# The causal mask of the layer-0 score scan: applied by VectorE while it takes the maximum, in place of a TensorE matmul

## The reference

```python
# layer 0
scores = jnp.einsum('bhqd,bhkd->bhqk', q, k) * hd ** -0.5
scores = jnp.where(jnp.tril(jnp.ones((t, t), bool)), scores, -jnp.inf)
attn = jax.nn.softmax(scores, axis=-1)
x = x + gate * (attn_times_v @ Wproj + bproj)        # then a gelu MLP of width 1024
# layer 1
energy = jnp.einsum('bhqd,bhkd->bhqk', q, k)
att = jax.nn.softmax(energy, axis=-1) / D ** 0.5
out = attn_times_v @ Wp.T + bp + hidden              # then a modulated norm, added
```

## Time and profile before

| what | value |
|---|---|
| median of 3 executions | 1383.65 us (1379.31 to 1385.65) |
| the profiled execution's own time | 1379.89 us |
| its span, first to last instruction | 1378.1 us |
| PE busy | 1242.5 us, 90%, 6604 matmuls |
| DVE busy | 868.4 us, 63%, 1779 instructions |
| ACT busy | 672.3 us, 49% |
| POOL busy | 278.5 us, 20% |
| mean granted PE clock | 0.952 |
| scan matmuls L933 | 1024, 342.7 us busy |
| mask matmuls L936 | 512, 112.6 us busy |
| reduces L738 | 1024, 556.4 us busy |

### The profile page before, as it was taken

How to read it: one execution, slowest core, us unless ns; L and a number is a source line. 1 busy time by engine, 2 the same in 40 slices (tenths; PEclk the granted TensorE clock), 3 DMA queues, 4 the chain that set the end, 5 groups by cost and what they waited for, 6 DMA issues and landing times.

```text
span 1378.1 us, 18596 instructions
## 1 busy us (share of the span) xinstructions
PE 1242.5 (90%) x6604; PEld 596.1 (43%) x6604; DVE 868.4 (63%) x1779; ACT 672.3 (49%) x1338; POOL 278.5 (20%) x378
## 2 busy tenths in 40 slices
PE   6687878999999998999899999999899998997786
PEld 4234443345344543446344543445344632453232
DVE  3553457654787467865787468865887477723664
ACT  1153224564555554655555565555456465555263
POOL 1123012120233012321132013311132012110002
PEclk9799988999999999999999999999999998999698
DMA  5603013130515024320515033510614050202101
GB/s 149 184 2 88 5 47 77 34 92 17 117 49 124 1 64 101 77 65 17 130 35 124 1 78 87 112 31 17 148 34 115 11 114 19 57 1 66 44 18 39
DMA packets 56118, 89.34 MB, mean 65 GB/s; under 512 B 9842, under 2 KB 20690, under 8 KB 56026
## 3 DMA queue, kind: packets, MB, share of 16 engines
q1 hardware_dynamic: 55006, 87.34, 26.4%
q10 hardware_dynamic: 1020, 0.81, 0.2%
HBM read 24.41 MB, written 4.70 MB: 21 GB/s over the span
## 4 chain that ended last, share of the span: by engine, by line
PE 69%; DVE 13%; ACT 6%; issue 2%; DMA 1%; POOL 1%; SPq 1%; ACTq 0%; DVEq 0%; POOLq 0%
PE DN L992 16%; PE OP L912 12%; PE SX L933 11%; PE SC L923 10%; DVE MX L738 9%; PE DN L1041 8%; PE DN L1017 7%; ACT E L599 4%; PE DN L1005 2%; PE SX L936 2%; DMA KS<-PART 1%; PE DN L1070 1%; DVE OUT L788 1%; SPq L476 1%; DVE PART L816 0%
## 5 line engine op out<-in xcount | busy, mean ns | idle before, releaser
L738 DVE TENSOR_REDUCE MX<-SX 128x1 f32<-128x512 f32 (+3 forms) x1024 | 556.4, 584 | 280.5 <-PE SX L936 174.0
L599 ACT ACTIVATE E<-SC 128x512 f32<-128x512 f32 (+3 forms) x1024 | 461.0, 523 | 383.6 <-PE SC L923 307.9
L933 PE MATMUL SX<-KS,QS 96*128 96x512 bf16 (+3 forms) x1024 | 342.7, 360 | 80.0 <-DVE MX L738 52.3
L923 PE MATMUL SC<-QS,KS 99*128 99x512 bf16 (+3 forms) x1024 | 280.8, 348 | 17.4 <-ACT E L599 10.1
L933 PEld LDWEIGHTS SX<-KS,QS 96*128 96x128 bf16 x1024 | 99.0, 98 | 294.7 <-DVE MX L738 172.9
L912 PE MATMUL OP<-E,V 128*32 128x512 f32 (+3 forms) x2048 | 216.5, 541 | 2.9 <-DVE X L808 1.4
L923 PEld LDWEIGHTS SC<-QS,KS 99*128 99x128 bf16 x1024 | 95.6, 99 | 164.8 <-ACT E L599 101.5
L517 POOL TENSOR_SCALAR_AFFINE_SELECT E<-E 128x512 f32<-128x512 f32 x128 | 85.7, 672 | 339.6 <-ACT E L599 339.6
L1041 PE MATMUL DN<-XT,W 128*128 128x512 f32 x256 | 123.7, 608 | 0.8 <-ACT HID L651 0.3
L1017 PE MATMUL DN<-XT,WQKV 128*128 128x512 f32 x256 | 121.8, 620 | 0.9 <-ACT XT L632 0.9
L992 PE MATMUL DN<-W,HID 128*128 128x256 f32 x512 | 117.1, 382 | 0.0
(11 more groups left out here) (92 smaller groups left out, 915.5 us busy)
## 6 DMA issues: line engine op xcount, KB each, us to landing
QS<-PART SPq DMA_DIRECT2D x96, 256.0 KB, 4.8
KS<-PART SPq DMA_DIRECT2D x96, 256.0 KB, 6.5
OC<-OE SPq DMA_DIRECT2D x56, 128.0 KB, 5.4
RB<-recip_sums SPq DMA_DIRECT2D x56, 128.0 KB, 2.6
XIN<-in_x SPq DMA_DIRECT2D x8, 512.0 KB, 4.2
ROW<-row_vectors SPq DMA_DIRECT2D x8, 512.0 KB, 3.6
out<-OUT SPq DMA_DIRECT2D x7, 512.0 KB, 3.2
W<-in_w SPq DMA_DIRECT2D x2, 1024.0 KB, 8.2
```

Source lines behind the costliest of these rows:

```text
L599: a.activation(E[:, at["tick"].index() % 3, j, lo:T], SC[(at["head"].index() + j) % 3][:, lo:T], ACT.Exp, scale=HD ** -0.5 if layer == 0 e ...
L738: v.reduce_max(MX[:, qt, h:h + 1], SX[at["scan"].index() % 2][:, 0:w], AX.X, negate=True)\
L923: t_.matmul(SC[(at["head"].index() + j) % 3][:, lo:T], KS[layer][0:ALL_ROWS, h, kt * P:kt * P + P], QS[layer][0:ALL_ROWS, h, lo:T], start= ...
L933: ins = t_.matmul(bank[:, 0:w], QS[layer][0:CUT_ROWS, h, qt * P:qt * P + P], KS[layer][0:CUT_ROWS, h, 0:w], start=True, stop=layer == 1)
```

## The change

The mask matmul goes. DVE's reduce of a layer-0 scan becomes a masked one: it adds `CAUSAL` to the scores, multiplies by -1 and takes the minimum, which is the negated maximum. It reads the scores in PSUM and the mask in SBUF, and writes the sums back over the scores in PSUM, where nobody reads them. `CAUSAL` grows from 128 to 896 columns, with zeros in the first 384, so that one slice of it fits every tile: the slice for query tile `qt` starts at `(3 - qt) * 128`. Layer 1 keeps its reduce.

```diff
-        CAUSAL = sb("CAUSAL", [P, P], BF16)
+        CAUSAL = sb("CAUSAL", [P, 2 * T - P], BF16)
...
-            g.affine_select(out=CAUSAL[:], in_=CAUSAL[:], compare_op=ALU.is_ge, fill=MASKED, base=0,
-                            pattern=[[-1, P]], channel_multiplier=1).then_inc(consts, 1)
+            g.affine_select(out=CAUSAL[:], in_=CAUSAL[:], compare_op=ALU.is_ge, fill=MASKED, base=T - P,
+                            pattern=[[-1, 2 * T - P]], channel_multiplier=1).then_inc(consts, 1)
...
-                v.reduce_max(MX[:, qt, h:h + 1], SX[at["scan"].index() % 2][:, 0:w], AX.X, negate=True)\
-                    .then_inc(scan_done, 1)
+                tile, most = SX[at["scan"].index() % 2][:, 0:w], MX[:, qt, h:h + 1]
+                if layer == 0:
+                    if (b, h, qt) == (0, 0, 0):
+                        dve.wait_ge(consts, N_CONSTS)
+                    seen = CAUSAL[:, (TT - 1 - qt) * P:(TT - 1 - qt) * P + w]
+                    ins = v.tensor_tensor_reduce(tile, tile, seen, scale=-1.0, scalar=-MASKED,
+                                                 op0=ALU.add, op1=ALU.min, accum_out=most)
+                else:
+                    ins = v.reduce_max(most, tile, AX.X, negate=True)
+                ins.then_inc(scan_done, 1)
...
                 ins = t_.matmul(bank[:, 0:w], QS[layer][0:CUT_ROWS, h, qt * P:qt * P + P],
-                                KS[layer][0:CUT_ROWS, h, 0:w], start=True, stop=layer == 1)
-                if layer == 0:
-                    ins = t_.matmul(bank[:, qt * P:w], ID16[:], CAUSAL[:], start=False, stop=True)
+                                KS[layer][0:CUT_ROWS, h, 0:w], start=True, stop=True)
                 ins.then_inc(scan_full, 1)
```

## The result

| what | before | after |
|---|---|---|
| median | 1379.54 us (7 executions) | 1393.62 us (7 executions, 1386.89 to 1399.09) |
| ratio | 1 | 1.0086, 95% interval 1.0054 to 1.0119 |
| profiled execution, its span | 1378.1 us | 1392.3 us |
| PE busy, matmuls | 1242.5 us, 6604 | 1245.6 us, 6092 |
| DVE busy, instructions | 868.4 us, 1779 | 896.4 us, 2291 |

The change makes the kernel 0.9% slower, 12 to 14 us. The forecast was 1372 us, faster. The measured time lies inside the stated range of 1356 to 1397 us, but that is luck: the upper part of the range stood there for a readout that waits for the pipe, and this did not happen. The kernel before was executed again beside the changed one; its median over all seven is 1379.54 us, lower than that of the first three.

The account below looks back on a forecast made before the run. PE was taken to bound the kernel. Six layer-0 stretches at -1.7 us (-10.4), the opening -1.7 and DVE's queue and late evictions +1 gave -11 us from 1383.65: 1372 us, range 1356 to 1397.

Parts of the forecast that it names:

- a readout that waits for the pipe: First rival, at each of 512 tiles: readout starts only after the main instruction leaves the pipe; +21 us, 1405 us; chance 0.20.
- What bounds the kernel: PE, busy 90% of the span; it runs freely in most of a layer-0 stretch, while DVE's loop paces the tail.
- The free part: First 43 tiles of a layer-0 stretch: 35 gain 0.06 us each, 8 waiting ones lose 0.02 each; sum -1.9 us.
- DVE's price: Per layer-0 tile, main instruction +0.006 us and readout step 0.074, taken as 0.08; +41 us of DVE over 512 tiles.
- The tail: Last 21 tiles of a layer-0 stretch, paced by the PE-DVE loop: +0.03 us per head of four tiles, +0.2 us.
- the walk: Step-by-step timing of one four-tile head in the tail: 2.09 us before, 2.12 us after.
- the sum: Six layer-0 stretches at -1.7 us, -10.4; opening -1.7; longer DVE queue and later evictions +1; layer 1 nothing; total -11 us.
- Layer 1 has no change: Layer-1 stretches were taken to keep their time, adding nothing to the total.
- The opening: First layer-0 stretch, 128 tiles: half of -4.2 us counted, -2.1, plus 0.4 for its 58 waits; sum -1.7 us.
- The half rate: Rival: DVE's main instruction runs at half rate, 0.53 us more per 512 tile; +62 us, 1446 us; chance 0.07.
- The hidden readout: Rival: DVE's readout is hidden whole under the main instruction; -26 us, 1358 us; chance 0.10.
- The gain given back at ACT: Rival: PE only reaches its score weight loads' waits for an exponential sooner; about -3 us, 1381 us; chance 0.13.

## Why the prediction was wrong

**What bounds the kernel** was right: PE, with a free regime and a dense tail in each layer-0 stretch.

**The free part** gained in every stretch, somewhat less than forecast: 7.8 us over six, 1.3 each, where -1.9 was written. Without a mask and with the plain reduce the six take 339.7 us in place of 349.9. So PE's part of the gain is 1.7 each (2.1 in the sum), and DVE's price there is 0.4 (0.2 in the sum).

**DVE's price** was right, slightly high: 0.05 in throughput and 0.07 in latency per tile, against 0.08 for both. The main instruction was costed 0.006 over the reduce and has 0.03. With PE's work kept, the whole price was about 7.6 us.

**The tail** was right in its period at full clock, or nearly so: from the start of one 256-column main instruction to the next the changed kernel has 680.26 to 682.44 and 689.17 to 691.28 us, 2.18 and 2.11, where the walk gave 2.12.

**The step that failed is the sum**, in two places: "A stretch: -1.9 + 0.2 = -1.7; six of them", and "Layer 1 has no change". The +0.2 for a tail was 2.5 to 3.1 us in four of the six tails and 1.7 in a fifth. Layer 1's zero was +8.1 us. The opening, forecast at -1.7, was +3.0. Both take PE's speed as given. Every step of PE in the rows came from stretches at a granted clock of 1.00, and the sum carried them over to a kernel in which PE does less. The clock depends on what PE does. The tail walk even showed how: its period stays at 2.12 us while 0.24 us of PE work per head leaves it. I read this as a gain that is merely not realised. It was a loss of PE's work just where the clock then fell. The kernel before gave the warning in its own trace: the opening stretch at 0.87, and two layer-1 stretches at 0.96. None of the rivals held this mechanism. In layer 1, four of the five stretches of the changed kernel take 1.5 to 5 us more than the 81.2 us at full clock. What stays open is why the removal and the longer reduce lose so much only together, and what decides in which tail the clock falls.

**The rivals.** The readout overlaps its main instruction by 0.08 us, so the first is out. The Trainium skill (VectorE: DVE Perf Modes, section The DRAIN you can't avoid) says that the next operation does not start until the pipe is empty, and in the same place that one which is not held back starts earlier. This trace shows the earlier start, 0.08 us before the recorded end, for the readout too. The half rate is out: 714 ns. The hidden readout is nearly true for throughput. The gain given back at ACT is out too: PE's weight loads of the scores wait 236 times for an exponential, 103.0 us in all, against 240 times and 101.5 us before.

## What to carry to other kernels

Work taken off TensorE was worth its time here only where TensorE then ran on, in the free parts. Where another engine paces TensorE, taking matmuls away saved nothing, and the granted clock fell there and in parts that the change never touched. Before such a change is costed, look at the granted clock by stretch; where it falls in some stretches and holds in others that are alike, a price measured at full clock needs a rival in which it falls in more of them. And test the two halves of a change alone: one half gained the forecast 11 us, the other cost 8, and together they lost 12. A reduction that writes a result back and needs a readout is cheap by itself, at 0.07 us a tile, and was still part of the loss.

## What the runs showed of the hardware

In the changed kernel 161 matmuls of 128 columns that add zeros took 0.8% off the time (1.0086 to 1.0009), while the same 161 with 8 columns did not (1.0111). Beside the plain reduce the same 161 cost 0.7% (0.9924 to 0.9996). 112 zero matmuls in layer 1 made even the kernel before faster (0.9971). Time at the low clock cost about a third of its length: the layer-1 stretch with 17.0 us of it took 86.2 us against 81.2. The executions of the changed kernel lie 12 us apart (1386.89 to 1399.09) with nothing changed between them, and their clocks differ too: 0.932 in the fastest, 0.922 in the slowest. The masked maximum, a DVE instruction reading and writing the same PSUM bank, costs as much per column as the reduce: 313 to 714 ns for 384 more columns is 1.04 ns a column, and 285 to 684 ns is the same.
